# Scan parameters, long filter and the mixer's weights in one block, with the filter's two halves of time on two halves of partitions

## Time and profile before

| what | us |
|---|---|
| median of 3 runs | 4767.65 (4763.98 to 4768.28) |
| the profiled execution | 4775.44 |
| its span, first to last instruction | 4773.7 |
| PE busy in the span | 4307.8 (90%) |
| DVE, POOL, ACT busy | 3254.1, 2349.4, 2160.8 |
| from the first instruction of the scan parameters (126.48) to the mixer's first load (322.67) | 196.19 |

### The profile page before, as it was taken

The page is one execution under the profiler, slowest core; times in us unless marked ns, Lnnn a source line. Parts: engine busy times, 40 slices in busy tenths (PEclk is TensorE's granted clock), DMA queues, the critical chain, the costliest instruction groups (busy, mean ns, idle before and its releaser), DMA issues. The chain is left out here.

```text
span 4773.7 us, 118783 instructions
## 1 busy us (share of the span) xinstructions
PE 4307.8 (90%) x39924; PEld 3574.9 (75%) x39924; DVE 3254.1 (68%) x6762; ACT 2160.8 (45%) x5049; POOL 2349.4 (49%) x3277
## 2 busy tenths in 40 slices
PE   5259999999999999999999999999978999989999
PEld 4128777777777777777777777777756888878888
DVE  8456666667676666666676666666644666658888
ACT  3124444444444444444444444444435666645555
POOL 3027666566655666566566656665520000006666
PEclk9669999999999999999999999999988999999999
DMA  8120111111111111111111111111007666643333
GB/s 271 78 79 27 33 47 37 38 41 37 47 37 33 46 37 45 37 35 45 37 41 40 37 45 35 35 47 37 30 29 193 181 185 179 181 124 101 105 104 97
DMA packets 369422, 347.40 MB, mean 73 GB/s; under 512 B 24665, under 2 KB 342937, under 8 KB 359833
## 3 DMA queue, kind: packets, MB, share of 16 engines
q1 hardware_dynamic: 352028, 323.88, 22.8%
q10 hardware_dynamic: 16896, 16.78, 1.0%
HBM read 231.91 MB, written 108.66 MB: 71 GB/s over the span
## 5 line engine op out<-in xcount | busy, mean ns | idle before, releaser
L733 PE MATMUL bank<-w_bc,xnT 128*128 128x512 f32 x3072 | 815.8, 408 | 40.2 <-POOL xnT L1054 40.2
L733 PEld LDWEIGHTS bank<-w_bc,xnT 128*128 128x128 f32 x3072 | 570.2, 192 | 180.3 <-issue 65.6
L936 ACT COPY turned_t<-bank 128x512 f32<-128x512 f32 x512 | 299.6, 585 | 860.8 <-PE bank L756 860.7
L1467 PE MATMUL p_yc<-sig,toep 64*64 64x256 f32 (+14 forms) x16384 | 539.5, 282 | 17.1 <-issue 13.9
L1062 POOL TENSOR_TENSOR steps<-upto,par 128x512 fp32r<-128x512 f32 x512 | 550.4, 1095 | 5.6 <-PE bank L742 5.6
L1467 PEld LDWEIGHTS p_yc<-sig,toep 64*64 64x64 f32 x16384 | 476.9, 132 | 92.7 <-issue 46.3
L1171 DVE TENSOR_TENSOR rot<-bank,par 128x512 f32<-128x512 f32 x512 | 350.6, 685 | 240.8 <-PE bank L733 162.5
L1071 POOL TENSOR_TENSOR turned_b<-rot 128x512 f32<-128x512 f32 x256 | 325.1, 1270 | 308.7 <-DVE rot L1172 308.3
L766 PEld LDWEIGHTS bank<-turned_t 128*128 128x128 f32 x2048 | 301.3, 214 | 127.6 <-issue 104.9
L766 PE MATMUL bank<-turned_t 128*128 128x128 f32 x2048 | 310.5, 301 | 93.5 <-issue 92.0
L1191 DVE TENSOR_TENSOR mix<-bank,decay 128x512 f32<-128x512 f32 x256 | 175.9, 687 | 300.4 <-PE bank L766 299.9
(11 more groups left out here) (259 smaller groups left out, 9741.2 us busy)
## 6 DMA issues: line engine op xcount, KB each, us to landing
toep<-taps_dram SPq DMA_DIRECT2D x256, 260.0 KB, 4.2
el<-el_dram SPq DMA_DIRECT2D x256, 128.0 KB, 3.0
xg<-arg_x SPq DMA_DIRECT2D x32, 512.0 KB, 5.0
xnT_dram<-xt_g ACTq DMA_DIRECT2D x32, 512.0 KB, 5.1
xnT_raw<-xnT_dram SPq DMA_DIRECT2D x128, 128.0 KB, 2.3
x_quad<-arg_x SPq DMA_DIRECT2D x32, 512.0 KB, 3.9
x_dram<-x_quad SPq DMA_DIRECT2D x32, 512.0 KB, 3.7
x0T_dram<-conv SPq DMA_DIRECT2D x32, 512.0 KB, 2.8
```

Source lines behind the costliest of these rows:

```text
L733: last = mm(p_bc[c][:, :], xnT[w.q % 2][p][:, k, :], w_bc[q][:, k, c * 1024 + g * W4:c * 1024 + (g + 1) * W4], start=(n == 0), stop=(n == ...
L936: s_.copy(turned_t[g][c][:, :], p_tr[:, :]).then_inc(s[f"copy_{BC[c]}"], 1)
L1467: last = mm(by_seq(p_y[p][c][odd * H:(odd + 1) * H, 0:2 * TILES])[:, :, first:], toep[n % SLOTS][c * H:(c + 1) * H, lag * H:(lag + 1) * H] ...
```

## The change

`scan_parameters`, `long_filter` and the weights' block become one block, `scan_and_filter`; the mixer's block follows it directly. What it does:

- **Loads.** SyncE issues twelve small loads (the filter's weights twice, on partitions 0 to 63 and 64 to 127) on one semaphore that all engines wait for in full, then the eleven weights. The raw weights go into space that is used later: `raw_bc` into `taps`, `raw_u` and `raw_in` into `params_all`. `decay` is loaded straight into `taps` when GpSimd says that the raw weights are no longer needed (`weights_done`).
- **Filter.** The first half of time stands on partitions 0 to 63, the second on 64 to 127, 1024 columns each, so that one instruction of VectorE or ScalarE does both. The three reductions stand between parts of the scan's work on VectorE; the third comes after the scan's parameters are complete.
- **Weights.** ScalarE rounds the `hi` parts after the filter's first sine; GpSimd forms the `lo` parts in six subtractions (by 128 rows of the input), each pair after its `hi`.
- **Writes into `params_all`** wait for `weights_done`. `taps` is stored in two parts, by 128 channels.
- PSUM: three tensors for the scan and one for the filter; the last matmuls of the filter use all four.

```diff
-def scan_parameters(nc, ctx, t):
+def scan_and_filter(nc, ctx, t):
...
+    h, r, m = sb("mlp_h", [128, HALF]), sb("mlp_r", [128, HALF]), sb("mlp_m", [128, HALF])
+    taps = sb("taps", [128, KT, TOK - 1 + SEQ])
+    raw_bc = taps[:, :, :].rearrange("p k n -> p (k n)")[:, 0:KT * 2048].rearrange("p (k n) -> p k n", k=KT)
...
+    LAYERS = ((w1, pos), (w2, h), (w3, h))
+    outs = ((ph, 0, 0), (pp[0], 0, 1), (pp[1], 1, 0), (pp[2], 1, 1))
...
         @block.sync
+            sp.dma_start(pos, t["pos"]).then_inc(s["small_in"], 16)
+            sp.dma_start(w1[:, :], t["mlp_w1"]).then_inc(s["small_in"], 16)
+            for half in range(2):
+                rows = slice(half * FILT, (half + 1) * FILT)
+                for dst, src in ((w2, "mlp_w2"), (w3, "mlp_w3"), (wo, "mlp_wo"), (freq_b, "freq_b")):
+                    sp.dma_start(dst[rows, :], t[src]).then_inc(s["small_in"], 16)
+            for dst, src in ((raw_bc, by_k("w_bc")), (raw_u, by_k("w_u")), (raw_in, by_k("in_w")),
...
+                sp.dma_start(dst, src).then_inc(s["weights_in"], 16)
+            sp.wait_ge(s["weights_done"], 1)
+            for k in range(KT):
+                sp.dma_start(taps[:, k, TOK - 1:], t["decay"][k * 128:(k + 1) * 128, :]).then_inc(s["weights_in"], 16)
+            sp.wait_ge(s["scan_dve"], PARAMS)
...
+            for k in range(KT):
+                sp.wait_ge(s["taps_out"], 2 * k + 2)
+                sp.dma_start(t["taps_dram"][k * 128:(k + 1) * 128, :], taps[:, k, :]).then_inc(s["stored"], 16)
+            sp.wait_ge(s["stored"], 64)
+        @block.gpsimd
...
+            pool.wait_ge(s["weights_in"], 16 * 11)
+            for k in range(4):
+                g_.tensor_scalar(w_out[:, k, :], w_out[:, k, :], rms_w[:, k:k + 1], None, ALU.mult)
...
+            for n, (raw, (hi, lo)) in enumerate(((raw_bc, w_bc), (raw_u, w_u), (raw_in, in_w))):
+                pool.wait_ge(s["weights_hi"], n + 1)
+                for k in range(KT):
+                    g_.tensor_tensor(lo[:, k, :], raw[:, k, :], hi[:, k, :].bitcast(F32), ALU.subtract)
+            pool.drain()
+            g_.memset(taps[:, :, 0:TOK - 1], 0.0)
+            pool.drain().then_inc(s["weights_done"], 1)
         @block.vector
+            dve.wait_ge(s["small_in"], 16 * 12)
...
+            reduce_layer(0)
+            dve.wait_ge(s["scan_act"], SOFT)
...
+            v_.tensor_tensor(omd[:, 0:COLS], arr["m2"][:, :], arr["dt"][:, :], ALU.mult)
+            dve.drain().then_inc(s["scan_dve"], 1)
+            reduce_layer(1)
+            dve.wait_ge(s["scan_pe"], CUMULATED)
...
+            dve.drain().then_inc(s["scan_dve"], 1)
+            dve.wait_ge(s["weights_done"], 1)
             v_.tensor_copy(col(P_A), as3(a_hi[:, :].bitcast(F32)))
...
+            reduce_layer(2)
+            dve.wait_ge(s["weights_in"], 16 * (11 + KT))
+            for n, (bank, k, half) in enumerate(outs):
+                dve.wait_ge(s["layer_out"], 4 + n)
+                c = slice(TOK - 1 + half * HALF, TOK - 1 + (half + 1) * HALF)
+                v_.tensor_tensor(taps[:, k, c], taps[:, k, c], bank[:, :], ALU.mult)
+                dve.drain().then_inc(s["taps_out"], 1)
         @block.scalar
...
+            act.wait_ge(s["reduced"], 1)
+            s_.activation(h[:, :], r[:, :], ACT.Sin).then_inc(s["sine"], 1)
+            act.wait_ge(s["weights_in"], 16 * 11)
+            for raw, (hi, lo) in ((raw_bc, w_bc), (raw_u, w_u), (raw_in, in_w)):
+                s_.copy(hi[:, :, :], raw).then_inc(s["weights_hi"], 1)
+            act.wait_ge(s["reduced"], 2)
+            s_.activation(h[:, :], r[:, :], ACT.Sin).then_inc(s["sine"], 1)
+            act.wait_ge(s["scan_pe"], SUMS)
+            act.wait_ge(s["weights_done"], 1)
...
         @block.tensor
+            def filter_layer(layer):
+                w, src = LAYERS[layer]
+                wait(pe, s["sine"], layer)
+                for half in range(2):
+                    rows = slice(half * FILT, (half + 1) * FILT)
+                    for q in range(2):
+                        c = slice(q * 512, (q + 1) * 512)
...
+                            last = mm(ph[rows, c], w[rows, :], src[rows, c], start=True, stop=True)
+                last.then_inc(s["layer_out"], 1)
...
+            for bank, k, half in outs:
+                rows = slice(half * FILT, (half + 1) * FILT)
+                for q in range(2):
+                    c = slice(q * 512, (q + 1) * 512)
+                    last = mm(bank[:, c], wo[rows, k * 128:(k + 1) * 128], h[rows, c], start=True, stop=True)
+                last.then_inc(s["layer_out"], 1)
```

More of the change, by code:

```diff
@@ L252, in _ @@
         def _(sp):
[L253 to L258 removed]
+            by_k = lambda name: t[name].rearrange("(k p) n -> p k n", p=128)
@@ L332, in _ @@
[L332 to L339 removed]
+            dve.wait_ge(s["scan_act"], SINES)
@@ L370, in _ @@
+            s_.activation(h[:, :], r[:, :], ACT.Sin).then_inc(s["sine"], 1)
         @block.tensor
         def _(pe):
-            pe.wait_ge(dve_done, 2)
-            for half in range(2):
-                c = slice(half * 512, half * 512 + 512)
-                c1 = slice(half * 512 + HEADS, half * 512 + 512 + HEADS)
-                nc.tensor.matmul(pp[0][:, c], t["upto"][:, :], arr["dth"][:, c], start=True, stop=True)
-                nc.tensor.matmul(pp[1][:, c], t["ones"][:, :], arr["dth"][:, c], start=True, stop=True)
-                nc.tensor.matmul(pp[2][:, c], t["nxt"][:, :], omd[:, c], start=True, stop=False)
-                last = nc.tensor.matmul(pp[2][:, c], t["wrap"][:, :], omd[:, c1], start=False, stop=True)
@@ L380, in _ @@
-            last.then_inc(pe_done, 1)
-            pe.wait_ge(dve_done, 3)
-            for half in range(2):
-                c = slice(half * 512, half * 512 + 512)
-                nc.tensor.matmul(pp[0][:, c], t["upto"][:, :], arr["a"][:, c], start=True, stop=True)
-                nc.tensor.matmul(pp[1][:, c], t["after"][:, :], arr["a"][:, c], start=True, stop=True)
-                last = nc.tensor.matmul(pp[3][:, c], t["ones"][:, :], arr["a"][:, c], start=True, stop=True)
-            last.then_inc(pe_done, 1)
@@ new lines, in _ @@
+            pe.wait_ge(s["small_in"], 16 * 12)
+            filter_layer(0)
+            filter_layer(1)
+            pe.wait_ge(s["scan_dve"], LOGS)
+            for q in range(2):
+                c = slice(q * 512, (q + 1) * 512)
+                mm(pp[0][:, c], t["upto"][:, :], arr["dth"][:, c], start=True, stop=True)
+                mm(pp[1][:, c], t["ones"][:, :], arr["dth"][:, c], start=True, stop=True)
+            pe.wait_ge(s["scan_dve"], OMD)
+            for q in range(2):
+                c, c1 = slice(q * 512, (q + 1) * 512), slice(q * 512 + HEADS, (q + 1) * 512 + HEADS)
+                mm(pp[2][:, c], t["nxt"][:, :], omd[:, c], start=True, stop=False)
+                last = mm(pp[2][:, c], t["wrap"][:, :], omd[:, c1], start=False, stop=True)
@@ new lines, in _ @@
+            last.then_inc(s["scan_pe"], 1)
+            filter_layer(2)
+            pe.wait_ge(s["scan_dve"], ANGLES)
+            for q in range(2):
+                c = slice(q * 512, (q + 1) * 512)
+                mm(pp[0][:, c], t["upto"][:, :], arr["a"][:, c], start=True, stop=True)
+                mm(pp[1][:, c], t["after"][:, :], arr["a"][:, c], start=True, stop=True)
+                last = mm(pp[2][:, c], t["ones"][:, :], arr["a"][:, c], start=True, stop=True)
+            last.then_inc(s["scan_pe"], 1)
```

359 lines of the change are left out of this document (140 added, 219 removed).

## The result

| | before | after |
|---|---|---|
| median | 4765.81 (4762.59 to 4768.28, 4 runs) | 4689.8 (4685.21 to 4696.2, 4 runs) |
| ratio, 95% interval | | 0.984 (0.9824 to 0.9855) |
| the profiled execution | 4775.44 | 4688.05 |
| its span | 4773.7 | 4686.3 |
| first issue of the changed part | 126.48 | 126.22 |

The change took 76.0 us off the median; 4686 had been forecast. The stretch that was rewritten is 84.7 us shorter, where the sum had said 81.7: 3.0 us more were gained in the block than forecast, and the medians show 8.7 us less than the block.

The account below looks back on a forecast made before the run. No engine bound the stretch; three serial blocks did. Merged chain 204.6 + contention 10 + tail 26.4 = 241.0 for the mixer's first load against 322.67, 81.7 less; median 4767.65 - 81.7 = 4686 us, range 4668 to 4700.

Parts of the forecast that it names:

- The bound: Stretch from token norm to mixer's first load: three blocks in a row, no engine the bound, 196.2 us.
- Small loads, 134.6: Block's start: twelfth small load starts some 5.5 us in and lands 2.6 later, at 134.6.
- Layer 0, 141.4: Filter's first matmuls on TensorE: eight records, one overlapped per change of part, 6.8 us to 141.4; bounds 7.6 and 4.2.
- Reductions of 7.1, three of them: Filter's reductions on VectorE: three instead of six, at 7.1 us each, on 128 partitions.
- Contention, 10: GpSimd's subtractions beside VectorE's scan work: whole instructions take turns, delay 6.9 to 10.7 us, taken as 10.
- the first ends as VectorE leaves it: GpSimd's first subtraction, started at about 154 during VectorE's reciprocal, was to end as VectorE leaves the reciprocal.
- Chunk totals, range reduction, writes: Scan parts on VectorE's chain: chunk totals 8.2 us, range reduction 12.2, writes into params 1.9, 9.1 and 3.1.
- Tail, 26.4: Block's end: reduction 7.1, sine 1.1, sixteen matmul records 12.9 with partial overlap, last store 5.3; 26.4 us in all.
- The clock's rise at 229.2, a rival of 5%: Tail matmuls: at 2.4 GHz the 13 records take 6 us less, time 4680; chance 5%.
- The mixer unchanged: Mixer behind the block: its own work doesn't change, so the stretch's end goes one to one into the total.
- the gain is given back later: Mixer, with tensors elsewhere in SBUF: its 3237 us would have to be 2.8% slower; chance 1%.
- The rival without contention (20%): GpSimd beside VectorE: engines meet only now and then, or GpSimd starts after the exposed part; time 4676; chance 20%.
- that of no overlap (17%): Filter on TensorE: halves don't overlap and the small loads land late; time 4690 to 4696; chance 17%.

Follow-up runs that it names:

- e8: Changed kernel with engines waiting for six small loads, not twelve, raw weights earlier, GpSimd's subtractions placed under VectorE's reciprocals, some on VectorE: 4665.56 us, ratio to before 0.9795.
- e11: Against e8: ScalarE's first sine precedes the weights' rounding, GpSimd starts with the first reciprocal and is given less under it: 4666.78 us, ratio to before 0.9791.
- e3: Changed kernel with the filter's last eight matmuls reordered, all four of the first half of time before those of the second: 4689.57 us (1 run).
- e1: Changed kernel with GpSimd's six lo subtractions removed and VectorE making three instead, behind omd: 4657.79 us (1 run).
- e9: Changed kernel plus unused VectorE reciprocals of 1408 columns behind its last product, before the block can end: 4679.52 us.
- e7: Changed kernel with most GpSimd subtractions placed under VectorE's two reciprocals, the second one moved, and one large subtraction on VectorE: 4671.84 us, ratio to before 0.9802.
- e6: Same program as e1 (lo subtractions on VectorE instead of GpSimd, against the changed kernel), timed five times: 4669.74 us, ratio to before 0.9796.

## Why the prediction was right, and by which errors

**The bound: right.** What ended the stretch was the chain of blocks, and the gain went into the total; the mixer's length was unchanged in the profiled pair (3262.5 and 3261.9).

**Small loads, 134.6: right** (134.68), but by two errors: the twelfth load started 6.45 us after the first, not 5.5, and was in use 2.0 after that, not 2.6. It is the step that e8 and e11 then shortened by 3 us.

**Layer 0, 141.4: too late by 3.0.** This step failed: "only one record of overlap is to be had for each change of part". The reduction started at 138.44, 3.7 us behind TensorE's start, even a little below the step's lower bound of 4.2, which was full overlap. e3 shows that an order with runs of four matmuls does lose overlap, 2.0 us in sixteen records; with runs of two nothing is lost.

**Reductions of 7.1, three of them: right** (138.44 to 145.53; 173.65 to 180.73; 215.82 to 222.9). Nor did VectorE wait for the sums or for `weights_done`: GpSimd's last instruction there ended at 172.9 against 174 said.

**Contention, 10: right in kind, too small.** The term was priced at 6.9 to 10.7 and taken as 10; e1 against after shows 13.3, outside these bounds. Mechanism and place came as told: dth and a are as long as GpSimd's instruction ahead of them and their own time. All six instructions waited, also the tensor_scalar (1.75 for 0.69) and the cast (2.29 for 0.68): by instruction 4.05, 4.30, 0.86, 1.06, 1.61 and 1.45. The step that failed is "the first ends as VectorE leaves it". GpSimd's start hangs on the weights' loads and came when said (153.67 for 154), but VectorE left the reciprocal at 154.0, 3 us earlier than in the plan, because layer 0 was 3.0 shorter. So dth met the whole of the first subtraction (4.05), where the plan had it wait 1.4 (to 158.4 from 157.0). Without that difference the sum is 10.7, where all six waiting was priced at 9.7; the 0 to 1 us for GpSimd's scaling of `w_out` was nothing, since that ran beside the reciprocal (148.61 to 152.25). So of the 3 us won in layer 0 nearly all were lost at once, by this sum over the rows; no run moved GpSimd's start alone. e11, where GpSimd starts with the reciprocal, shows the other side of it. The Trainium skill's page "SBUF — State Buffer", section "Who interferes with whom", says that the single-input kind takes the lock too; that kind was not in any row of before, and e1 against after agrees with the page.

**Chunk totals, range reduction, writes: right.** 8.1, 12.8 and 14.0 us were measured for 8.2, 12.2 and 14.1. The params store was issued at 215.75 for 214.6, and it was hidden.

**Tail, 26.4: too long by 4.5.** From 215.82 to 237.73 are 21.9. The failed assumption on overlap again: matmuls and products took 9.1 (224.11 to 233.2), not 12.9. The clock's rise at 229.2, a rival of 5%, came in part: it shortened the matmuls by 0.9 us, and the end by no more than that, since VectorE's products were the last by then. The last store and the block's end took 4.5, not 5.3, near the bound of 4.3 from the earlier trace rows.

So the forecast of 241.0 for the mixer's load was 3.3 too late by this sum: 3.0 for layer 0 and 4.5 in the tail too much, 3.3 of contention and about 1 of small gaps too little. The first and the third belong together, as told; the tail's is what is left.

**The mixer unchanged: right in the profile, but not a safe step.** The profiled pair differs by 87.4 us (84.7 of it the block), the medians by 76.0, since the profiled execution of before was 9.6 above its median and that of after 1.8 below its own. Where the other executions differ from the profiled ones can't be placed, as they leave no trace, but the slower ones have the lower granted clock. e9 shows that an edit that lengthens the block by 5 us can come out 10 us shorter, with the mixer's code untouched. The rival "the gain is given back later" had been given 1% and a slowdown of 2.8% to decide the sign; at its true size, some 10 us either way, it should have widened the range of the time rather than stood as a case.

**How close the total came is in part luck.** 4686 against 4689.8: the median of before was 1.8 lower than the one that the forecast started from, the block gave 3.0 more, and the medians showed 8.7 less than the block. That is 4.8 one way and 8.7 the other, of which 3.9 are left.

The rival without contention (20%) is refuted by the rows, that of no overlap (17%) likewise. The mean clock in the tail was 0.61 from 224.0 to 230.6: 0.50 for the first 5 us, and at the upper level from 229.2 on, as told above.

## What to carry to other kernels

Short stages in a row are worth merging when each is load, chain, store: the halving alone gave 11 of the 85 us here, and the other 73 came only with the merged block. When work is moved to an idle GpSimd, look at what VectorE does at that time: six subtractions that cost VectorE 7.4 us cost it 13.3 on GpSimd beside elementwise work, and nothing beside a reciprocal. And when a short stage ahead of a long loop is edited, compare the loop's length too: an edit of 5 us can come out as 10 the other way (e9).

## What was not expected of the hardware

- Matmuls on different 64-row halves ran fully side by side although each half had two in a row: 16 records in 6.3 us; with four in a row 8.3 (e3). In both the clock rose from 0.50 to 1.00 near 229.2 to 229.7.
- VectorE's reciprocal of 1024 columns takes 6.55 us with GpSimd's two-input instructions under it and without them (e7, e11), while tensor_scalar, cast and tensor_tensor all wait.
- After a stop of TensorE of about 3 us the granted clock is 0.50 for 3 us or for 6. Where it is for 6, another 3.4 us at 0.50 follow half way through the pass, behind a stop of 1.5 us that has no such effect in the other passes; a pass of the mixer costs 102 us with these and 99 without. How many passes are of which kind differs between kernels with the same mixer, and between two executions of one program (9 in e1, 11 in e6), and moves a kernel of 4690 us by some 10.
